# The order of the expert slots turned round: nine of 128 rows first, then fifteen of 256 rows

## The reference, cut to what matters

```
h = signature(x) @ W.T + b                       # depth-4 path signature, 128 wide
h = h + attention(layernorm(h))                  # 8 heads
xf = layernorm(h)                                # 4096 tokens x 128
e  = argmax(xf @ gate_w.T)                       # one of 8 experts per token, weight 1
y  = w2[e] @ (silu(w1[e] @ xf) * (w3[e] @ xf))   # hidden width 512, the token's own expert only
y  = y + gelu(xf @ sw1.T) @ sw2.T                # the shared expert, for all tokens
return h + y
```

## Time and profile before

| | |
|---|---|
| runs | 646.2, 646.62, 649.11 us, median 646.62 |
| the profiled execution: its own time | 645.78 us |
| its span in the trace | 644.0 us |
| PE busy | 617.4 us (96%) |
| DVE, ACT, POOL busy | 428.9, 290.1, 321.4 us |
| the first expert transposes on PE | 530.57 us from the span's start |
| PE's last product ends | 632.86 us (631.71 + 1.15) |
| the last scatter starts on POOL | 634.94 us |

### The profile page before, as it was taken

One profiled execution on the slowest core, in us unless ns is written; L12 is line 12 of the kernel. 1 busy time (PEld: TensorE's weight loads), 2 busy tenths in 40 slices (PEclk: granted clock), 3 DMA queues, 4 the chain that ended last, 5 costly groups with the idle time before them and its releaser, 6 DMA issues.

```text
span 644.0 us, 13364 instructions
## 1 busy us (share of the span) xinstructions
PE 617.4 (96%) x4085; PEld 519.6 (81%) x4085; DVE 428.9 (67%) x1093; ACT 290.1 (45%) x640; POOL 321.4 (50%) x336
## 2 busy tenths in 40 slices
PE   5989999999999999999999999999989999999993
PEld 3767888887888887888888787888768899999992
DVE  6976777766777766777776778788556535666450
ACT  4324444444344455344444444444464545666331
POOL 2455544454554455554455455445854501566663
PEclk9989999999999999999999999999999999999997
DMA  8611443345553334343334434111235712444330
GB/s 302 247 76 34 100 98 82 82 102 110 101 128 82 82 86 119 89 104 92 82 82 111 102 94 103 38 37 39 69 98 176 203 49 62 55 54 56 43 47 2
DMA packets 69902, 59.80 MB, mean 93 GB/s; under 512 B 6513, under 2 KB 58609, under 8 KB 69489
## 3 DMA queue, kind: packets, MB, share of 16 engines
q1 hardware_dynamic: 63232, 55.21, 33.2%
q0 software_dynamic: 6640, 4.22, 4.9%
HBM read 16.79 MB, written 26.30 MB: 67 GB/s over the span
## 4 chain that ended last, share of the span: by engine, by line
PE 83%; DVE 8%; POOL 3%; issue 3%; ACT 1%; DMA 0%; SPq 0%; ACTq 0%; DVEq 0%; POOLq 0%
PE bank L1300 77%; PE bank L1511 2%; PE bank L1356 2%; POOL z L492 1%; POOL sorted_rows L507 1%; DVE z L921 1%; PE bank L1611 1%; PE bank L1405 1%; POOL z L494 1%; PE bank L1360 0%; PE bank L1414 0%; DVE mask L1104 0%; DMA h<-x_prev 0%; POOL rstd L501 0%; DVE rowmax L1046 0%
## 5 line engine op out<-in xcount | busy, mean ns | idle before, releaser
L1300 PE MATMUL bank<-whigh,uth 128*128 128x512 f32 x512 | 168.2, 409 | 1.2 <-DVE lowt L815 1.2
L1300 PEld LDWEIGHTS bank<-whigh,uth 128*128 128x128 f32 x512 | 92.4, 190 | 26.8 <-issue 7.5
L1300 PE MATMUL bank<-whigh,utl 128*128 128x512 f32 x256 | 101.9, 398 | 0.0
L581 POOL DMA_INDIRECT out<-xvo,ids x39 | 61.3, 1572 | 65.0 <-ACT xvo L770 58.1
L501 POOL TENSOR_TENSOR rstd<-rstd,powers 128x1 f32<-128x1 f32 x64 | 35.2, 550 | 113.9 <-DVE rstd L908 65.9
L492 POOL TENSOR_TENSOR z<-z 128x512 f32<-128x512 f32 x32 | 42.2, 1319 | 70.6 <-DVE z L921 70.6
L1300 PE MATMUL bank<-xT,qkw 128*128 128x128 f32 x512 | 63.4, 277 | 0.0
L656 ACT ACTIVATE prob<-prob 128x512 f32<-128x512 f32 x32 | 20.2, 633 | 93.3 <-DVE prob L1048 93.3
L1300 PEld LDWEIGHTS bank<-xT,qkw 128*128 128x128 f32 x512 | 59.6, 192 | 0.7 <-issue 0.4
L1300 PEld LDWEIGHTS bank<-whigh,utl 128*128 128x128 f32 x256 | 48.4, 189 | 11.4
L487 POOL TENSOR_TENSOR e3l<-e,e3h 128x512 fp32r<-128x512 f32 x31 | 41.1, 1325 | 26.9 <-DVE xn L942 26.4
(11 more groups left out here) (236 smaller groups left out, 1357.8 us busy)
## 6 DMA issues: line engine op xcount, KB each, us to landing
sorted_rows<-blank SPq DMA_DIRECT2D x24, 709.5 KB, 5.9
xvp<-xvo SPq DMA_DIRECT2D x128, 128.0 KB, 2.3
w<-w_t SPq DMA_DIRECT2D x1, 4096.0 KB, 12.0
w<-w_high SPq DMA_DIRECT2D x4, 512.0 KB, 6.5
x_columns<-x2t SPq DMA_DIRECT2D x32, 64.0 KB, 1.6
xg_in<-x_columns SPq DMA_DIRECT2D x8, 256.0 KB, 5.6
levels<-w_t SPq DMA_DIRECT2D x1, 2048.0 KB, 8.8
out<-h SPq DMA_DIRECT2D x8, 256.0 KB, 2.2
```

Of the source, the lines that this page charges most:

```text
L581: nc.gpsimd.indirect_dma_start(out=out[:, :], out_offset=bass.IndirectOffsetOnAxis(ap=ids[:, tile:tile + 1], axis=0), in_=y[:, 2 if j == S ...
L1300: return T.matmul(out_, lhsT, rhs, start=start, stop=stop)
```

## The change

Slots 0 to 8 become the nine singles and slots 9 to 23 the fifteen pairs. The number of each kind, the rows that each reads and every product stay. `size`, `unit`, the slices of the index arithmetic and the constants follow; the weights of slots 0 to 2 are now made by `expert_weights` on DVE, with a wait for the scatters into `sorted_rows` ahead of them (the buffer lies in x2); the slot made between the halves of the last shared `down` is a single; the last slot is a pair.

```
@@
+SMALL = SORTED - 2 * BIG
 def size(j):
-    return 2 if j < BIG else 1
+    return 1 if j < SMALL else 2
 def unit(j):
-    return 2 * j if j < BIG else BIG + j
+    return j if j < SMALL else 2 * j - SMALL
@@ scalar
-            for j in range(2):
-                expert_hi(j)
...
-            expert_hi(2)
-            for n in range(2):
-                silu(n)
+            silu(0)
             for j in range(SLOTS):
                 if j + 1 < SLOTS:
                     silu(unit(j + 1))
                 if j + 2 < SLOTS:
                     rows_transposed(j + 2)
-                if j + 1 < BIG:
+                if SMALL <= j + 1 < SLOTS:
                     silu(unit(j + 1) + 1)
-                if j + 3 < BIG:
+                if SMALL <= j + 3 < SLOTS:
                     expert_hi(j + 3)
                 result(j)
@@ vector
+            d.wait_ge(scattered, 16 * TILES)
             for j in range(2):
-                expert_lo(j)
+                expert_weights(j)
             add_shared(GROUPS - 2, 0)
             for j in range(2):
                 keep_ids(j)
-            for j in range(2):
-                rows_lo(j)
-            for n in range(2):
-                gate(n)
+            gate(0)
+            expert_weights(2)
             add_shared(GROUPS - 1, 1)
-            d.wait_ge(scattered, 16 * TILES)
-            expert_lo(2)
             for j in range(SLOTS - 1):
                 gate(unit(j + 1))
-                if j + 2 < BIG:
+                if SMALL <= j + 2 < SLOTS:
                     rows_lo(j + 2)
-                if j + 1 < BIG:
+                if SMALL <= j + 1:
                     gate(unit(j + 1) + 1)
-                if j + 3 < BIG:
+                if j + 3 < SMALL:
+                    expert_weights(j + 3)
+                elif j + 3 < SLOTS:
                     expert_lo(j + 3)
-                elif j + 3 < SLOTS:
-                    expert_weights(j + 3)
                 if j + 2 < SLOTS:
                     keep_ids(j + 2)
@@ tensor
             down(GROUPS - 1, 1, range(2))
-            pair_up(0, 0)
-            pair_up(0, 1)
+            tile_up(0)
             down(GROUPS - 1, 1, range(2, GROUP))
             for j in range(SLOTS):
-                if j + 1 < BIG:
+                if j + 1 < SMALL:
+                    tile_up(j + 1)
+                elif j + 1 < SLOTS:
                     pair_up(j + 1, 0)
-                elif j + 1 < SLOTS:
-                    tile_up(j + 1)
                 if j + 2 < SLOTS:
                     rows_in_columns(j + 2)
-                if j + 1 < BIG:
+                if SMALL <= j + 1 < SLOTS:
                     pair_up(j + 1, 1)
```

More of the change, by code:

```diff
@@ L50 @@
 BIG = 15
-SLOTS = BIG + SORTED - 2 * BIG
+SMALL = SORTED - 2 * BIG
+SLOTS = SMALL + BIG
 PAIR = 2 * P
@@ L746, in expert_hi @@
                 e = a.value_load(exp_i[0:1, j:j + 1], min_val=0, max_val=EXPERTS - 1)
-                if j >= 4:
+                if j >= SMALL + 4:
                     a.wait_ge(up3_psum, unit(j - 4) + 2)
@@ L1201, in skip @@
                 return V.tensor_tensor(skipped[:, slots, :], upt[:, slots, :], spread(gap, 1, shape), ALU.mult)
-            bigs, smalls = slice(0, BIG), slice(BIG, SLOTS)
+            smalls, bigs = slice(0, SMALL), slice(SMALL, SLOTS)
             ended(bigs, end_p)
@@ L1221, in _ @@
             rstep(V.tensor_tensor(row_f[:], row_f[:], slot_row, ALU.add))
-            rstep(V.scalar_tensor_tensor(row_f[:, smalls], taken[:, 0:1].to_broadcast([P, SLOTS - BIG]), float(PAIR),
+            rstep(V.scalar_tensor_tensor(row_f[:, smalls], taken[:, 0:1].to_broadcast([P, SMALL]), float(PAIR),
                                          row_f[:, smalls], ALU.mult, ALU.add))
@@ L1234, in expert_weights @@
                 e = d.value_load(exp_i[0:1, j:j + 1], min_val=0, max_val=EXPERTS - 1)
-                if j - 2 >= BIG:
+                if j >= 2:
                     d.wait_ge(up3_psum, unit(j - 2) + 1)
@@ L1242, in expert_lo @@
                 e = d.value_load(exp_i[0:1, j:j + 1], min_val=0, max_val=EXPERTS - 1)
-                if j >= 4:
+                if j >= SMALL + 4:
                     d.wait_ge(up3_psum, unit(j - 4) + 2)
-                d.wait_ge(pair_hi, j + 1)
+                d.wait_ge(pair_hi, j - SMALL + 1)
                 remainder(whigh[:, 1, j % 4, :], w13[:, bass.ds(e, 1), :].rearrange("p o i -> p (o i)"),
@@ L1608, in rows_in_columns @@
                     pe.wait_ge(rT_sb, j - 1)
-                    pe.wait_ge(rT_lo, min(j - 1, BIG))
+                if j - 2 >= SMALL:
+                    pe.wait_ge(rT_lo, j - 1 - SMALL)
                 for n in range(size(j)):
@@ L1614, in pair_up @@
             def pair_up(j, half_):
-                n = unit(j) + half_
-                if n >= 2:
-                    pe.wait_ge(hid_done, n - 1)
+                n, k = unit(j) + half_, (unit(j) + half_) % 2
+                pe.wait_ge(hid_done, n - 1)
                 if half_ == 0:
-                    pe.wait_ge(pair_lo, j + 1)
-                    pe.wait_ge(rT_lo, j + 1)
+                    pe.wait_ge(pair_lo, j - SMALL + 1)
+                    pe.wait_ge(rT_lo, j - SMALL + 1)
                 x = (pairTh[:, j % 2, :], pairTl[:, j % 2, :])
@@ L1625, in pair_up @@
                         w = [whigh[:, p, j % 4, col(m * HC + 2 * half_ + c)] for p in range(2)]
-                        last = three(B[1 + 2 * half_ + m][:, col(c, PAIR)], w, x)
+                        last = three(B[1 + 2 * k + m][:, col(c, PAIR)], w, x)
                     last.then_inc(done, 1)
@@ L1631, in tile_up @@
                 n, k = unit(j), unit(j) % 2
-                pe.wait_ge(hid_done, n - 1)
-                pe.wait_ge(w13_copied, j - BIG + 1)
+                if n >= 2:
+                    pe.wait_ge(hid_done, n - 1)
+                pe.wait_ge(w13_copied, j + 1)
                 pe.wait_ge(rT_sb, j + 1)
@@ L1737 @@
         "steps": on_all(np.concatenate([EXPERTS - np.arange(EXPERTS), P * np.arange(TILES),
-                                        np.arange(BIG), np.arange(SLOTS - BIG), PAIR * np.arange(BIG),
-                                        P * np.arange(SLOTS - BIG), TILES * P * np.arange(EXPERTS)])
+                                        np.arange(SMALL), np.arange(BIG), P * np.arange(SMALL),
+                                        PAIR * np.arange(BIG), TILES * P * np.arange(EXPERTS)])
                         .astype(np.float32)),
```

## The result

Four executions of the changed kernel took 652.17, 653.56, 653.99 and 655.6 us, median 653.77; before 646.2 to 649.11, median 647.12. The ratio is 1.010, with a 95% interval of 1.0063 to 1.0136: slower by 1.0%, some 6.6 us. The forecast was 650.6 and a range of 648.2 to 652.8. The sign was right, the size was not.

The account below looks back on a forecast made before the run. PE's string of products bounds the expert stage. Head 0, turn +0.7, last gate -0.2, end +3.2 and +0.7 sum to +4.4 us: 650.2 by the profiled execution, 651.0 by the median, forecast 650.6, range 648.2 to 652.8.

Parts of the forecast that it names:

- PE's own work: Expert products on PE: fifteen pairs and nine singles keep number and pace, clock stays 1.00; change 0.
- The head: First slots, among the last shared products: weights, rows and scatters come in time; 0, up to 0.5 us for a late load.
- the 1.2 us in hand: Slot 2's rows: load lands at the latest at 536.6, transposes come at about 537.8; in time by 1.2 us.
- The turn: Singles to pairs, slots 7 to 10: PE waits twice, 0.7 us in all, between 0.2 and 2.5.
- gate and rows_lo: Ahead of pair_up(9, 0): PE waits about 0.4 us for DVE's gate(8) and rows_lo(9), range 0.2 to 0.6.
- counted from slot 8's transpose: Loop 6 timing: rows copied by 0.6, weights cast by 1.64, keep_ids done at 3.15, slot 10's load landed at 6.05 us.
- the load: Ahead of slot 10's transposes: PE waits 0.3 us with a median load of 2.1 us, 2.1 us with the slowest.
- rival 3: Slot 10's load as late as the slowest seen: 2.1 us in place of 0.3, so +6.2, 652.0; chance 0.10.
- the clock: PE's granted clock: 1.00 in both stretches, so nothing to be had there; no term in the sum.
- The end: Behind PE's last product: four scatters on POOL instead of two, +3.2 us; the last landing later, +0.7 us.
- Rival 2: Closing runs from the end of PE, ACT and DVE, hiding the scatters: not slower, 645.6 to 646.3; chance 0.04.
- The gap of 0.2 us for the last gate: Ahead of the last down: PE's 0.2 us wait for the gate goes with a pair's 16 products; -0.2 us.

Follow-up runs that it names:

- the shifted stream: Changed kernel with 64 more wait instructions at the head of PE's list, moving PE's instruction fetches: 657.56 to 660.02 us, median 658.29.
- 654.25: One execution of the changed kernel measured once more, unedited: 653.43 to 654.33 us, median 654.26, ratio to before 1.0118.
- the gap filled: Changed kernel with 14 more products on PE ahead of slot 10's transposes, into a bank overwritten next: 651.71 to 653.51 us, median 651.94.

## Why the prediction was wrong in size

- **PE's own work, 0: right.** With the second gap gone and 0.27 us left of the first the experts take 102.3 us in the new order too, the singles' period is 2.79 us (555.20 to 557.99), and the granted clock through the experts is 1.00 in that trace and in the one of before.
- **The head, 0: right.** No gap in slots 0 to 8. Slot 2's load took 3.57 us and its transposes did not wait, as the 1.2 us in hand had it.
- **The turn, 0.7 us: here it failed.** Both waits were named at their place with the releasers that they had, and both were priced too low.
  - gate and rows_lo, 0.4: measured 0.79. The step "counted from slot 8's transpose: ACT copies the rows by about 0.6, casts slot 9's weights by 1.64" left out the load of the expert number into ACT's register, by which the cast came 0.55 us later. DVE works in order, so the low part, gate(8) and rows_lo came late, and slot 10's load by about 0.5. The rows show this chain; that the gap falls to 0.27 us once the casts are made early and rows_lo stands first agrees with it, but that run changed both at once.
  - the load, 0.3: measured 1.85, of which 0.40 is left when no fetch stands beside it (the shifted stream) and 1.45 is the fetch. The issue was about 0.5 us late, but PE came 0.4 later too, so the 0.3 was nearly right for a load of 2.1 us. The step "lands 2.1 after that by the median" is the one that failed: the load took 3.60. I treated 3.9 us as a rare draw, 1 in 24, and gave rival 3 a chance of 0.10. The landings read were 12 and not 24, and 2 of the 24 loads were that slow. It is no draw either: the slow loads have a fetch of instructions among their packets, and at slot 10 the fetch came 1.25, 1.26 and 1.30 us behind the issue in all three traces that leave PE's list alone up to there and SP's issue where it was. The chance should have come from asking what stood beside the slow one; the trace of before had the q8 packet there.
  - the clock: missing from the sum. I wrote that "nothing is to be had there" and never asked what PE's standing would do to it. It cost about 1.6 us in the one execution in which it was seen to fall. Three traces have both gaps (652.17, 654.25, and 651.40 with one scatter less) and only the second has a fall; with the gap filled the median was 1.8 to 2.3 us lower. So it is shown that it happens and what it costs there. That it is the difference between the executions at 652 and those at 654 is suggested and not shown.
- **The end, +3.2 and +0.7: right, a little high.** Measured 2.91 and 0.46, the latter between the 0.7 of the sum and the 0.15 that the prediction gave as an estimate beside it. The order of before with four scatters pays 3.4 us, the changed order with three saves 1.8. Rival 2 is refuted. The Trainium skill (Runtime: NRT & Kernel Launch, section "The ~15µs preamble/postamble breakdown") lets the closing begin when all engines are done, and the runs agree: from the last landing to the span's end it was 6.35 us before, 6.35 after, 6.3 with one scatter less (643.34 to 649.61) and 6.5 with four in the order of before (641.29 to 647.81).
- **The gap of 0.2 us for the last gate, -0.2: right.**

The execution first profiled is rival 3 in kind (the same load late) and in time (652.0 forecast, 652.17 measured). That the two times agree so well is in part luck: 0.53 us ahead of the slots and 0.14 more at the turn stand against 0.53 less at the end. The median lies 1.6 us above it. A fall of the clock costs as much, but how much of the median is the clock stays open.

## What to carry to other kernels

The cost of an order is read at its seams and not in its periods: both orders have the same 102.3 us of products, and nearly all the difference is in one turn and one tail. Put at the end of the list the unit whose result needs the fewest instructions of the slowest queue behind it, and at a turn between two kinds of unit check each helper's lead anew. Before a slow DMA in a trace is called chance, look at what else ran on its engines: a fetch of instructions comes at the same place in every run, and a wait that it makes longer can cost as much again in TensorE's clock, as it did in one execution here.

## What was not expected of the hardware

- One 16 KB instruction fetch (q8) takes 0.9 to 1.8 us of one DMA engine. A 129 KB load of a pair's rows that is spread over all 16 landed after 3.0 to 4.1 us with a fetch that started 0.75 to 1.85 us behind its issue, and after about 2.1 without; all but one of its 16 landings were in time. With a fetch of 8 KB (q14) 1.1 to 1.3 us behind the issue, slot 23's load took 2.8 to 3.3 us.
- After 2.9 us of standing in two pieces (0.8 and 2.1 us) the granted clock fell to the lower level at 564.5 for 3.4 us in one execution; after 2.6 and 2.7 us in two pieces it did not in two others.
- 64 instructions with two semaphore waits each, all already met, cost PE 6.1 us, nearly 0.1 us an instruction.
- The register load of an expert number on ACT begins 0.83 us before the cast that needs it (555.52 to 556.35) and costs 0.57 us where only a copy of 0.27 us runs beside it; beside a silu of 0.60 us (544.90) the cast follows after 0.05.
